# Attention with three of eight probability tiles transposed by DMA instead of TensorE

## What is computed

```python
xn = _layernorm(x, axis=-1)
x = x + attention(xn, ...) + ffn(xn, ...)
# attention
qkv = (x @ qkv_w.T).reshape(Bb, Ss, 3, H, D)
q = _rope(q, c, s); k = _rope(k, c, s)
scores = jnp.einsum('bhqd,bhkd->bhqk', q, k) * SCALE
kb = -p * jnp.log1p(a * dist)
attn = jax.nn.softmax(scores + kb[None], axis=-1)
out = jnp.einsum('bhqk,bhkd->bhqd', attn, v)
return out.transpose(0, 2, 1, 3).reshape(Bb, Ss, H * D) @ out_w.T
```

## Time and profile before

| | |
|---|---|
| median of 3 runs | 1337.12 us (1335.97 to 1337.2) |
| profiled execution, device time | 1339.31 us |
| its span | 1337.5 us |
| PE busy | 1216.2 us, 91% |
| DVE busy | 1098.9 us, 82% |
| ACT busy | 985.9 us, 74% |
| POOL busy | 798.0 us, 60% |
| mean granted clock of PE | 0.968 |

### The profile page before, as it was taken

How to read it: one execution, slowest core, us unless ns; L and a number is a source line. 1 busy time by engine, 2 the same in 40 slices (tenths; PEclk the granted TensorE clock), 3 DMA queues, 4 the chain that set the end, 5 groups by cost and what they waited for, 6 DMA issues and landing times.

```text
span 1337.5 us, 33943 instructions
## 1 busy us (share of the span) xinstructions
PE 1216.2 (91%) x13412; PEld 938.0 (70%) x13412; DVE 1098.9 (82%) x2166; ACT 985.9 (74%) x1831; POOL 798.0 (60%) x628
## 2 busy tenths in 40 slices
PE   5630999997699999999999999999999999999995
PEld 5620788895267777777777777777777777777764
DVE  7864799994388888888888888888888888888894
ACT  2775688882388777777778777877778777877773
POOL 3044000001788887886788788877778887886600
PEclk9975899998899999999999999999999999999998
DMA  8625666661445444444553454355445444444411
GB/s 267 237 62 187 219 236 234 234 212 40 117 123 141 104 111 127 120 117 115 147 154 98 112 151 104 96 141 142 117 130 146 105 112 127 120 118 113 135 41 48
DMA packets 172685, 182.47 MB, mean 136 GB/s; under 512 B 78066, under 2 KB 150783, under 8 KB 172528
## 3 DMA queue, kind: packets, MB, share of 16 engines
q1 hardware_dynamic: 160256, 160.03, 41.9%
q0 software_dynamic: 4352, 12.41, 2.7%
q10 hardware_dynamic: 7920, 7.87, 2.0%
HBM read 109.12 MB, written 54.56 MB: 122 GB/s over the span
## 4 chain that ended last, share of the span: by engine, by line
PE 71%; ACT 1%; DMA 1%; issue 1%; DVE 1%; SPq 0%; ACTq 0%; DVEq 0%
PE ps_t L1307 17%; PE ps_o L1323 13%; PE ps_x L1263 13%; PE ps_s L1296 8%; PE ps_s L1297 8%; PE ps_x L1283 7%; PE ps_x L1273 6%; ACT prob L1111 1%; DMA kswap<-qk_dram 0%; DMA qk_dram<-parts 0%; DMA ot<-ctx_parts 0%; ACT proj L1073 0%; ACT prob L1073 0%; DVE ctx_parts L1193 0%; ACT pt_hi L1087 0%
## 5 line engine op out<-in xcount | busy, mean ns | idle before, releaser
L1172 DVE SCALAR_TENSOR_TENSOR pt_lo<-ps_t,pt_hi 128x1024 f16<-128x1024 f32 x256 | 312.6, 1221 | 129.1 <-ACT pt_hi L1087 129.1
L1207 DVE CUSTOM_DVE_ANT_0 neg<-ps_s,strips,score_scale 128x512 f32<-128x512 f32 x512 | 361.7, 743 | 8.1 <-PE ps_s L1297 8.0
L1111 ACT ACTIVATE prob<-neg,neg_max 128x512 f32<-128x512 f32 x512 | 362.6, 712 | 0.0
L1087 ACT ACTIVATE pt_hi<-ps_t 128x1024 f16<-128x1024 f32 x256 | 261.9, 1023 | 128.5 <-PE ps_t L1307 126.5
L1307 PE MATMUL ps_t<-ident,prob 128*128 128x128 f32 x2048 | 269.4, 273 | 4.3 <-ACT prob L1111 4.2
L1307 PEld LDWEIGHTS ps_t<-ident,prob 128*128 128x128 f32 x2048 | 234.3, 141 | 39.1 <-issue 10.6
L1323 PE MATMUL ps_o<-val_hi,pt_hi 128*128 128x64 f16 x2048 | 206.0, 193 | 1.8 <-DVE pt_lo L1172 1.7
L1323 PE MATMUL ps_o<-val_hi,pt_lo 128*128 128x64 f16 x2048 | 206.2, 193 | 0.0
L1323 PE MATMUL ps_o<-val_lo,pt_hi 128*128 128x64 f16 x2048 | 206.2, 193 | 0.0
L1296 PE MATMUL ps_s<-qk 128*128 128x512 f16 x512 | 195.4, 382 | 6.0 <-DMA kswap<-qk_dram 5.6
L1297 PE MATMUL ps_s<-kswap,qk 128*128 128x512 f16 x512 | 194.9, 381 | 0.0
(11 more groups left out here) (186 smaller groups left out, 2565.0 us busy)
## 6 DMA issues: line engine op xcount, KB each, us to landing
raw<-in_L_ffn_w_dram SPq DMA_DIRECT2D x32, 1024.0 KB, 5.1
qk_dram<-parts SPq DMA_DIRECT2D x128, 256.0 KB
qk<-qk_dram SPq DMA_DIRECT2D x32, 1024.0 KB, 5.6
kswap<-qk_dram SPq DMA_DIRECT2D x64, 256.0 KB, 6.5
xa<-in_L_attn_x_dram SPq DMA_DIRECT2D x8, 512.0 KB, 6.4
xt_dram<-xth SPq DMA_DIRECT2D x8, 512.0 KB, 5.1
slots_dram<-zeros SPq DMA_DIRECT2D x4, 1024.0 KB, 8.3
xa<-slots_dram SPq DMA_DIRECT2D x16, 256.0 KB, 5.3
```

The costliest lines, as they stand in the source:

```text
L1087: nc.scalar.activation(pt[0][:, (l - 1) % 2].rearrange("p q k c -> p q (k c)"), ps_t[l % 2][:], ACT.Copy, scale=P_SCALE).then_inc(turned_h ...
L1111: nc.scalar.activation(prob[:, l % 2, q, :], neg[:, l % 2, q, :], ACT.Exp, bias=neg_max[:, 2 * (l % 2) + q:2 * (l % 2) + q + 1], scale=-1. ...
L1172: nc.vector.scalar_tensor_tensor(out=pt[1][:, (l - 1) % 2].rearrange("p q k c -> p q (k c)"), in0=ps_t[l % 2][:], scalar=P_SCALE, in1=pt[0 ...
L1207: nc.vector.tensor_tensor_reduce(neg[:, l % 2, q, :], ps_s[q][:], strips[:, h, start:start + S], score_scale[:, 0:1], 3.0e38, ALU.add, ALU ...
```

## The change

In the slots k = 1, 4 and 6 of each group (`DMA_TURNS`; 95 of the 256, as slot 254 is left out) PE does not transpose. There ACT and DVE make the high and low halves of `prob` before it is turned, in `prob_parts` (`prob_high`, `prob_low`), and SP turns both with one DMA transpose into `pt` (`turn_probs`). For this the values of a slot are computed three slots later instead of two, on all slots; `prob` and `pt` have three buffers; `neg` is gone, the reductions write into `prob` and the exponentials work there in place. ACT makes the exponentials of a slot ahead of the high half of the one before. The low halves stand in DVE's queue by a fixed table: `pair_lo` of the remaining slots 0, 3, 5 at the head of slots 3, 6 and the next 0, of 2 and 7 behind the reductions of slot 4 and of the next group's slot 1; `prob_low` behind the reductions of the next slot. Context reads move from l % 4 = 2 to 3, `context_lo` to the slot behind. `rot` loses its buffer for the second half: each half is rotated and split before the next. `move` is cut into `move_out` and `move_in`, between which SP turns a tile and the context.

```diff
+DMA_TURNS = (1, 4, 6)
...
-        rot = sb("rot", [P, 2, 2, S])
+        rot = sb("rot", [P, 2, S])
...
-        neg = sb("neg", [P, 2, 2, S])
-        prob = sb("prob", [P, 2, 2, S])
+        prob = sb("prob", [P, 3, 2, S])
-        pt = [sb(f"pt_{n}", [P, 2, 2, TPB, P], F16) for n in ("hi", "lo")]
+        pt = sb("pt", [P, 3, 2, 2, TPB, P], F16)
+        prob_parts = sb("prob_parts", [P, 2, 2, S], F16)
...
+        def by_dma(s):
+            return s % 8 in DMA_TURNS and s < NB * PAIRS - 2
...
+            def turn_probs(s):
+                n = dma_slots(s)
+                wait(sp, pv_done, s - 2)
+                sp.wait_ge(prob_lo, n + 1)
+                sp.dma_start_transpose(pt[:, s % 3].rearrange("p a q k c -> p (a q k) c"),
+                                       prob_parts[:].rearrange("p a q s -> p (a q s)")).then_inc(turned_by_dma, 16)
...
+            def group(b, j):
+                first = PAIRS * b + 8 * j
+                if first:
+                    turn_probs(first - 2)
+                    before = divmod(4 * b + j - 1, 4)
+                    if ahead(*before):
+                        move_out(*ahead(*before)[:2])
+                turn_probs(first + 1)
+                if first:
+                    turn_context(*before)
+                if first + 8 < NB * PAIRS:
+                    move_in((4 * b + j + 1) // 2, (j + 1) % 2)
+                if j == 1 and not is_last(b):
+                    load_routes(b + 1)
+                turn_probs(first + 4)
...
# POOL: each half w is rotated, copied and split before the next
             def step(F, fills):
                 for w in range(2):
                     rotate(F, w, fills + 2 * w + 2)
-                for w in range(2):
                     if F > 1:
                         high(F, w)
                     low(F, w)
...
# ACT
+            def prob_high(s):
+                n = dma_slots(s)
+                act.wait_ge(exp_done, 2 * s + 2)
+                wait(act, turned_by_dma, 16 * n)
+                nc.scalar.activation(prob_parts[:, 0], prob[:, s % 3], ACT.Copy, scale=P_SCALE).then_inc(prob_hi, 1)
...
-                    nc.scalar.activation(prob[:, l % 2, q, :], neg[:, l % 2, q, :], ACT.Exp,
+                    nc.scalar.activation(prob[:, s % 3, q, :], prob[:, s % 3, q, :], ACT.Exp,
...
+                if by_dma(s):
+                    prob_high(s)
+                if s and not by_dma(s - 1):
+                    pair_hi(b, l)
...
# DVE
+            def prob_low(s):
+                dve.wait_ge(prob_hi, dma_slots(s) + 1)
+                nc.vector.scalar_tensor_tensor(out=prob_parts[:, 1], in0=prob[:, s % 3], scalar=P_SCALE, in1=prob_parts[:, 0],
+                                               op0=ALU.mult, op1=ALU.subtract).then_inc(prob_lo, 1)
...
+                if s % 8 in (0, 3, 6) and s >= 3:
+                    pair_lo(s - 3)
+                if s % 4 == 0 and s >= 8:
+                    context_lo(s // 4 - 2)
+                if s % 4 == 3 and s >= 7:
+                    read_context(s // 4 - 1)
...
+                if s % 8 in (1, 4) and s >= 2:
+                    pair_lo(s - 2)
+                if s and by_dma(s - 1):
+                    prob_low(s - 1)
                 kind = slot_kind(b, l)
                 if kind:
                     read_fill(kind, b, l, fills_before(b, l))
-                if l or not is_first(b):
-                    pair_lo(b, l)
-                if l % 4 == 3 and not (is_first(b) and l == 3):
-                    context_lo(b, l - 1)
...
# PE
-                if l or not is_first(b):
+                if s and not by_dma(s - 1):
                     transposes(b, l)
-                if l >= 2 or not is_first(b):
-                    values(b, l)
+                if s >= 3:
+                    values(s - 3)
```

More of the change, by code:

```diff
@@ L938, in _, with move_out @@
         def _(sp):
-            def move(n, r):
+            def move_out(n, r):
                 F = 2 * n + r
-                wait(sp, scored, 16 * (F - 1))
                 sp.wait_ge(parts_lo, 2 * F + 2)
@@ L946, in move, with move_in @@
                                  parts[32 * h:32 * h + 32].rearrange("p w a f s -> p (w a f) s")).then_inc(parts_written, 16)
+            def move_in(n, r):
+                F = 2 * n + r
+                wait(sp, scored, 16 * (F - 1))
                 sp.wait_ge(parts_written, 64 * F + 64)
@@ L967, in load_routes @@
                 sp.dma_start(gate[:], gate_dram[b]).then_inc(routes_loaded, 16)
-            def batch(b):
-                for j in range(4):
-                    if j or not is_first(b):
-                        turn_context(b, j - 1)
-                    if j == 1 and not is_last(b):
-                        load_routes(b + 1)
-                        sp.wait_ge(filled, fills_before(b, 14))
-                        load_x(b + 1)
-                    if ahead(b, j):
-                        move(*ahead(b, j)[:2])
-            load_routes(0)
-            move(0, 0)
-            move(0, 1)
-            over_batches(batch)
+            def group(b, j):
[13 more added lines that the diff above has]
+                turn_probs(first + 4)
+                if j == 1 and not is_last(b):
+                    sp.wait_ge(filled, fills_before(b, 14))
+                    load_x(b + 1)
+            load_routes(0)
+            move_out(0, 0)
+            move_in(0, 0)
+            move_out(0, 1)
+            for b in range(NB):
+                for j in range(4):
+                    group(b, j)
             turn_context(NB - 1, 3)
@@ L995, in rotate @@
                 wait(pool, turned_parts, done)
[L996 removed]
+                wait(pool, parts_lo, 2 * F + w)
                 for half, (first, second, op) in enumerate(((cos, sin, ALU.subtract), (sin, cos, ALU.add))):
[L998 removed]
+                    nc.gpsimd.tensor_tensor(rot[:, half, :], proj[:, w, 0, :], first[:], ALU.mult).then_inc(turned_parts, 1)
                     wait(pool, turned_parts, done + 3 * half)
@@ L1328, in slot @@
             def slot(b, l):
+                s = PAIRS * b + l
                 j, k = divmod(l, 8)
@@ L1352, in _ @@
             transposes(NB - 1, PAIRS)
-            values(NB - 1, PAIRS)
-            values(NB - 1, PAIRS + 1)
+            for s in range(NB * PAIRS - 3, NB * PAIRS):
+                values(s)
             pe.wait_ge(ctx_turned, 16 * 4 * NB)
```

108 lines of the change are left out of this document (56 added, 52 removed).

## The result

The changed kernel is slower: a median of 1436.49 us (1424.18 to 1441.02), against 1337.16 for the kernel before on the same chip, a ratio of 1.071 (95% interval 1.063 to 1.080). Forecast were 1305 and a range up to 1330. The profiled execution, the fastest of four, took 1424.18 us with a span of 1422.3. To land is to have the data in place; times to landing are counted from issue.

What follows compares the result with a forecast made beforehand. PE was taken to bound 30 of 32 groups. Each saves 2.64 - 1.46 = 1.18 us, thirty of them 35 us; less 3 us at the start, -32 us: 1305 us from a median of 1337, range 1264 to 1330.

Steps and rivals of the forecast that it cites:

- "At nothing" for the transposes in SP's queue: SP and DMA queue: three more transposes per group, with Q and K moves shifted around them, cost no time.
- my 3.7: DMA queue: slot 4's transpose has its data in place 3.7 us after issue.
- margin of 1.6: Slot 4's transpose: data there at 7.2 us, wanted by PE in slot 7 at 8.81, so 1.6 us spare.
- my slower rival: Slot 4's transpose lands behind `move_in`, 9 us after `prob_low`; PE waits 3.7 us in slot 7; 1373 us; chance 0.12.
- the point from which it turns slower: Slot 4's transpose: the kernel becomes slower than before once the landing takes over 7.9 us.
- ACT: nothing to pay: ACT's high half of a DMA slot: copy from SBUF 1.05 us against 1.02 from PSUM; the new order only moves waits.
- The low half, 1.75 us: DVE's `prob_low`, two SBUF inputs: 1.15 us at least, 1.75 with half a POOL operation before it; POOL held up about 1 us.
- PE's wait for `yacc`, 1.46 us a group: PE's first fill of a group waits 1.46 us for DVE to read slot 7's output fill, behind two `prob_low`.
- Start +3 us: Start of attention: a single `rot` buffer delays rotation and splitting, costing 2.4, say 3 us.
- The clock of 1.0 "as before": PE's granted clock stays at 1.0, since PE 95% busy from 1280 us on had kept it.
- The 79 us that PE saves: PE: eight transposes go in three of eight slots, 2.64 us per group, 79 us over 30 groups.
- the queue is empty long before, by my walk: Argument against the slower case: Q and K loads land in some 6 us, before slot 4's transpose starts.

Runs made afterwards that it cites:

- e9: Changed kernel with the loads of Q and K cut to 128 of 2048 columns from the third group on: 1341.12 us (0.998).
- e16: Changed kernel with a second `prob_parts` buffer used in turn, in the memory of the low QKV weights, which the fills leave out: 1367.01 us (1.020).
- e6: Changed kernel with POOL's operations on Q and K cut to 64 of 512 columns from the third group on: 1376.23 us (1.024).
- e3: Changed kernel with only slots 1 and 6 turned by DMA, slot 4 given back to PE: 1389.80 us (1.037).
- e14: Changed kernel with only slots 1 and 4 turned, `pair_lo` two slots behind, fill read before `prob_low`, full work: 1352.13 us (1.010).
- e8: Changed kernel, but DVE reads the fill ahead of `prob_low`: 1407.88 us (1.048).
- e17: Changed kernel with a second `prob_parts` buffer (low QKV weights left out) and the fill read ahead of `prob_low`: 1406.08 us (1.046).
- e4: Changed kernel with only slots 1 and 4 turned by DMA, slot 6 given back to PE: 1360.22 us (1.013).
- e18: Changed kernel with second `prob_parts` buffer, fill read first, short loads of Q and K and short POOL work: 1324.61 us (0.988).
- e15: Changed kernel with slots 1 and 4 turned, `pair_lo` two slots behind, fill read first, loads cut to 128 of 2048 columns: 1350.99 us (1.007).
- e10: Changed kernel with loads at 128 of 2048 columns and POOL's operations at 64 of 512 from the third group on: 1306.38 us (0.974).
- e11: Changed kernel with only slot 1 turned by DMA, `pair_lo` two slots behind, fill read before `prob_low`, full work: 1325.50 us (0.989).
- e7: Changed kernel with the loads of Q and K issued from ACT's queue behind the exponentials of slot 3: 1592.91 us (1.187).
- e1: Changed kernel with `move_in` issued ahead of the transposes of slot 1 and of the context in SP's queue: 1438.35 us (1.072).

## Why the prediction was wrong

**"At nothing" for the transposes in SP's queue: the step that failed.** I walked the group and let the loads land "before the transpose of slot 4 starts". In the trace they are issued only 3.2 us ahead of it (3.9 in the median), and land after it is issued. For `move_in` stands behind the context's transpose, and SP waits for the low half of the context, one slot later now, 90.2 us in 31 times. The transpose took 7.4 us in the group shown against my 3.7; less the margin of 1.6 that would be 2.1 us of waiting for PE, and it was some 1.5 (51.2 us in 33 times). Without the loads' weight (e9) the time is 95 us lower. The mechanism is that of my slower rival, at 7.4 us and not 9. Its price was too low even so: 1373 us, where 1436 was measured. There I had placed the point from which it turns slower at 7.9 us; it turned slower below it, for the reason that follows.

**"ACT: nothing to pay".** I priced ACT's copy (1.05 us forecast, 1057 ns measured) and not its new wait, `wait(act, turned_by_dma, 16 * n)`: one buffer, three users. That was in the diff. Slot 4's transpose is wanted by slot 6's high half, 3.9 us after its issue in the group shown (755.38), where even a transpose that meets nothing (3.7 us) is just in time; PE wants it 2 us later. e16 prices it: 69 us of 99 by the medians, 56 of 73.5 in the attention part. The rule to add a wait's queue to the sum I applied to DVE and PE, not to ACT.

**The low half, 1.75 us: right.** Measured 1218 / 1675 / 2999 ns (least, median, longest), mean 1726, and POOL was held up nearly as said: it is busy for 879.4 us instead of 798.0, 0.9 us for each of the 95 low halves where I had said 1, and its operation `rot<-proj,sin` takes 1704 ns in the mean, 1289 before. The Trainium skill, page "SBUF — State Buffer", section "SBUF: two separate sides", gives the exclusion for two SBUF inputs; e6 agrees with it, 1226 ns once POOL is busy for only 245 of 920 us (380 to 1300). Its worth was under-rated, however: e3, without a late transpose, is still at 1.037, and e14 at 1.010. I had counted only one place where DVE meets PE, the output fill of slot 7. Reductions and exponentials behind a slow low half are another, and e8, e14 and e17 show that it takes the first one's place.

**PE's wait for `yacc`, 1.46 us a group: the number came out (47.6 us over 28 times, 1.7 each), in part by luck.** I had it from two slow low halves alone. In the group shown DVE was late because it had stood still for 2.45 us behind the late transpose, which my sum did not hold. Without the late transposes the wait is 22.9 us (e9), with short low halves 29.3 (e6), and with the second buffer 0.2 (e16), although the low halves there take 1.6 us.

**Start +3 us.** Measured +11.3, of which some 8 are PE's clock in this execution. From 320 to 350 us the granted clock was 0.50 in the changed kernel (the lower level, 1.2 GHz) and 0.89 in the one before:

```profile
320.00:350.00 30.00, 23.47 (x56) 7.00 (x57) 9.45 (x14) 6.57 (x10) 2.14 (x2) 0.50 0.09 26
```

e4, e6 and e18, with the same code there and clocks of 0.50 to 0.52, reach the first exponential at 378.2 to 379.1; e3, e14, e15 and e16, at 0.84 to 0.89, at 366.8 to 371.4, which is 1 to 6 us behind the 365.45 before. So the +3 holds at about the same clock. Why PE starts this stretch at the lower level in some executions I did not settle.

**The clock of 1.0 "as before".** From 380 to 1300 us the granted clock was 1.00 before and 0.97 in the changed kernel, with stretches of 20 us at 0.83 (520 to 540 us, for one); a matmul of a Q or K fill took 396 ns in the mean there instead of 379. By busy time per matmul that is some 11 us for these fills, an estimate. e9 and e14, without the long waits for the transposes, had 1.00. My sum had no term for it.

**The 79 us that PE saves** are the upper bound that I took for PE alone. No version reached more than 46.5 of them in the attention part (e10). Its median group takes 28.2 us, and what holds the last 0.8 us of it is not isolated; the largest wait of its PE is for `yacc`, 22.4 us in 28 times, and ACT still waits 30.9 us for the single buffer.

**Chances.** 0.12 for the slower rival was too low. It rested on "the queue is empty long before, by my walk", and in the trace the loads were still under way when the transpose was issued.

Not tried: a second buffer of `prob_parts` (4 KB per partition) with all the work kept; short POOL work with the transposes on time by distance, as in e14; and e11's single slot with the table of the changed kernel.

## What to carry to other kernels

A DMA transpose that is cheap by its own latency (3.7 us) keeps the DMA engines busy for much of that time (2.3 us here); before moving work to it, lay out for each turned tile the distance in time to the other transfers of the loop, and ask for a distance of a whole landing (7.8 us here was enough, 3.9 was not). List every wait of the change, by buffer, with the time from its producer to its next writer: a single staging buffer turned some 3.7 us of lateness in each group into 69 us of the kernel. And where a moved operation reads twice from SBUF beside a busy GpSimd, take its lengthened time for everything queued behind it, not for the one consumer that comes first to mind; here one turned slot in eight paid a third of what PE saved, and three cost time.

## What the runs showed of the hardware

Loads and transposes that run at once from two queues go worse than one behind the other: in e7 the DMA engines moved 303 GB/s from 834 to 838 us, and 116 in the next six, while being as busy (share 0.95 and 1.26), and the context's transpose took 14.0 us in the median. In the changed kernel, from 757 to 758 us, when the transpose had the engines to itself, they moved 289:

```profile
757.00:758.00 1.00, 0.39 (x4) 0.10 (x1) 0.52 (x2) 0.00 (x0) 0.94 (x2) 1.00 1.27 289
```

The transpose of e14 issued at 720.58 us met nothing; the three microseconds from 721 to 724 hold its traffic, and their shares add up to 2.3 us:

```profile
721.00:722.00 1.00, 0.69 (x3) 0.21 (x4) 1.00 (x5) 0.79 (x3) 0.92 (x2) 1.00 0.20 47
722.00:723.00 1.00, 0.94 (x6) 0.42 (x7) 0.97 (x3) 1.00 (x4) 0.99 (x1) 1.00 1.27 290
723.00:724.00 1.00, 1.00 (x11) 0.91 (x10) 1.00 (x4) 1.00 (x2) 0.94 (x1) 1.00 0.84 187
```

The share can pass 1, as these rows show, so it is not the same as elapsed time. SP is held longer by a transpose behind other transfers: 1.6 us with the queue empty, 5.72 in e1.
